# Unread products on TensorE ahead of and inside the lead of block attention

## The chip, the cores and the metric

One core of one Trainium2 chip. The metric is device time of one execution in microseconds (us), as the median of several runs. The kernel before took 1211.43 us (median of 3, from 1207.39 to 1212.15).

## The reference

Two transformer layers on x of shape (2, 1024, 128), each an attention and a feed-forward part behind a layer norm, with residual additions. The first layer has 16-head rotary attention and a mixture of eight experts chosen by argmax. The second is where the change lies:

```python
q = (hidden @ Wq.T + bq).reshape(B, S, 16, 8)          # k and v likewise; B, S = 2, 1024
scores = einsum('bihd,bjhd->bhij', q, k) / sqrt(8)
blk = arange(S) // 32
allowed = blk[:, None] >= blk[None, :]
scores = where(allowed, scores, 0)                     # zero, not minus infinity
probs = softmax(scores, axis=-1)
ctx = einsum('bhij,bjhd->bihd', probs, v)
x = x + ctx @ Wo.T + bo                                # then a gated feed-forward part
```

Masked scores are 0, so each row's softmax has a share from later keys, which the kernel takes from suffix sums of the values.

## The kernel before, in words

The kernel runs three functions one after the other: `rotary_attention` (to some 714 us), `experts`, and `block_attention` (from about 823 us). Engines have their own instruction streams and meet only by semaphores and at the ends of a `Block`.

`block_attention` has two blocks. The first normalizes x, projects it with Wq, Wk and Wv in eight 512-column products (`project`, L1175) and four quarters of values (`project_v`, L1183), and sums values for the later keys (`sum_values`). On TensorE (PE) its last work is `project_v(3)`, at k = 7 of the loop at L1200. VectorE (DVE) still splits k into a high and a low part, adds the value bias and scales the sums (`keep_sums`, L1300) before the block ends.

The second block holds the attention proper, in 8 groups of 4 heads (2 batches by 4). Each group has 20 fills and 24 steps. A fill is a pair of score blocks, for two heads, with queries on the partitions: `query_scores(f, 0)` and `(f, 1)` (L1536), products on 61 or 64 rows, the first head's in partitions 0 to 63, the second's in 64 to 127, each into one of three 512-column PSUM banks. DVE takes the row maximum of each bank (`row_max`, L1744, the reduction at L1754) and frees it; a fill may not start before the bank of three blocks ago is free (L1545). The maxima give each row's shift, which goes back through PE transposes (`shift_transposes`, L1501), ScalarE (ACT) and small transfers of SyncE (SP) into the moving operand. A step is a pair of score blocks with keys on the partitions (`key_scores`, L1512), of which ACT takes the exponential (`exps`, L1693, L1700); after two of four steps PE multiplies them with the values (`values`, L1562, L1575), four heads side by side in the bank `out_ps`, and at the end of a half adds the suffix product (L1579).

Every engine goes through the same list of jobs j = -1 to 207. Fills run ahead of steps by LEAD = 22 fills. So j = -1, the lead, is 22 fills with nothing else on PE but eight transposes ahead of fill 12:

```python
def fills_at(j):
    return range(0, LEAD) if j < 0 else range(fills_by(j - 1), fills_by(j))
```

From j = 0 on, the order within a job is key scores, fills, then at j = 5, 9, 13, ... two values products.

`fixed` is a constant f32 table of 128 partitions in SBUF; `w_ps` is a PSUM bank of the first block, read last when the normalized x of quarter 2 is kept; `out_ps` is first written by `values(0, 0)` with start=True.

Of the kernel before, what the change touches and what calls it, by code (L numbers as in the profile page):

```python
# [10 lines left out]
P = 128  # L11
# [1031 lines left out]
def block_attention(nc, core, operands, q_rows, k_rows, W_r, W_k, W_v, mu_r, mu_k, out):  # L1043
# [6 lines left out]
    with ExitStack() as st:  # L1050
# [4 lines left out]
        suffix, fixed = operands.suffix, operands.fixed  # L1055
# [18 lines left out]
        def sum_values(to, b):  # L1074
# [5 lines left out]
                                           start=kt == 4 * half, stop=kt == TB - 1)  # L1080
            return ins

        def keep_sums(src, b):

            own = fixed[:, 640:768].rearrange("p (h d) -> p h d", h=H1)
            for half in range(2):
                ins = nc.vector.tensor_tensor(suffix[:, b, half, :, 0:DH1], src[:, half * P:half * P + P].rearrange("p (h d) -> p h d", h=H1), own, ALU.mult)
            return ins
# [19 lines left out]
        with ExitStack() as st2:  # L1108
# [7 lines left out]
            w_ps = ps2("w", [P, 512])  # L1116

            def transpose_weights(pe):
                pe.wait_ge(operands.weights_loaded, 64)
                for i in range(4):  # L1120
                    ins = nc.tensor.transpose(w_ps[:, i * D:i * D + D], w[:, i, :], core.ident[:])
                ins.then_inc(wT_ready, 1)
# [21 lines left out]
            with nc.Block() as block:  # L1144
                @block.sync
                def _(sp):
                    sp.wait_ge(stack_ready, 2)
                    store_rows(sp, 0, 0, slice(0, HG), q_stored[0])
                    sp.wait_ge(stack_ready, 4)
                    store_rows(sp, 1, 0, slice(0, HG), k_stored[0])  # L1150
                    sp.wait_ge(q_stored[0], STORED)
                    load_pair(sp, q_still[0], q_rows, 0, 0, first_loaded[0])
                    sp.wait_ge(k_stored[0], STORED)
                    load_pair(sp, k_cur[0], k_rows, 0, 0, first_loaded[0])
                    load_pair(sp, q_still[0], q_rows, 0, 1, first_loaded[1])
                    load_pair(sp, k_cur[0], k_rows, 0, 1, first_loaded[1])
                    load_moving(sp, 0)
# [6 lines left out]
                @block.tensor  # L1164
                def _(pe):
                    def turn_normed(b):
                        for q in (2 * b, 2 * b + 1):
                            pe.wait_ge(xn_ready, q + 1)
                            if q == 3:
                                pe.wait_ge(full_ready, 1)  # L1170
                            for t in range(4 * q, 4 * q + 4):
                                ins = nc.tensor.transpose(turned_ps[q][:, t % 4 * P:t % 4 * P + P], xn[:, t, :], core.ident[:])
                            ins.then_inc(xnT_ready, 1)

                    def project(k):  # L1175
                        i, c = ORDER[k]
                        if k % 4 < 2:
                            pe.wait_ge(xT_kept, c + 1)
                        if k >= DEPTH:
                            pe.wait_ge(full_ready, k - DEPTH + 1)  # L1180
                        nc.tensor.matmul(s_ps[k % DEPTH][:], w_T[:, i, :], core.xT[:, c * 512:c * 512 + 512], start=True, stop=True).then_inc(proj_ready, 1)

                    def project_v(q):  # L1183
                        if q >= 2:
                            pe.wait_ge(v_added, q - 1)
                        for t in range(4 * q, 4 * q + 4):
                            ins = nc.tensor.matmul(v_ps[q % 2][:, t % 4 * D:t % 4 * D + D], core.xT[:, t * P:t * P + P], w_T[:, 2, :],
                                                   start=True, stop=True)
                        ins.then_inc(v_ready, 1)

                    transpose_weights(pe)
                    turn_normed(0)
                    pe.wait_ge(wT_copied, 1)
                    for k in range(4):
                        project(k)
                    for q in range(2):
                        project_v(q)
                    turn_normed(1)
                    pe.wait_ge(xT_kept, 4)
                    for k in range(4, 2 * DEPTH):  # L1200
                        project(k)
                        if k == 5:
                            pe.wait_ge(operands.fixed_loaded, 16)
                            pe.wait_ge(v_added, 2)
                            sum_values(sums_ps, 0).then_inc(sums_ready, 1)
                        if k >= 6:
                            project_v(k - 4)

                @block.scalar
                def _(act):  # L1210
# [112 lines left out]
        out_ps = ps("out", [P, 512])  # L1323
# [28 lines left out]
        def live(j):  # L1352

            return 0 <= j < GROUPS * STEPS
# [5 lines left out]
        def fills_at(j):  # L1360

            return range(0, LEAD) if j < 0 else range(fills_by(j - 1), fills_by(j))
# [71 lines left out]
        def fill_of(f, x):  # L1434
            m, i = f // FILLS, f % FILLS
            kind, hp = (i % 4, i // 4) if i < 8 else (i // 2, i % 2)
            return m, KINDS[kind], hp, x

        with nc.Block() as block:
# [60 lines left out]
            def _(pe):  # L1500
# [35 lines left out]
                def query_scores(f, x):  # L1536
                    m, (t, lo, hi), hp, x = fill_of(f, x)
                    n = bank["fill", f, x]
                    if m == 0 and f in (0, 4) and x == 0:
                        pe.wait_ge(operands.first_loaded[hp], LOADED)  # L1540
                    if m and f % FILLS == 0 and x == 0:
                        pe.wait_ge(still_loaded[m % 2], LOADED * (m // 2 + m % 2))
                        pe.wait_ge(k_loaded[m % 3], LOADED * (m // 3 + (m % 3 > 0)))
                    if n >= 3:
                        pe.wait_ge(bank_free, n - 2)  # L1545
                    parts = [(t, lo, hi, 0)]
                    if t < 2:
                        parts.append((t + 4, 4, t + 5, (hi - lo) * P))
                    for t, lo, hi, at in parts:
                        own = hi == t + 1  # L1550
                        rest = (hi - lo - own) * P
                        if rest:
                            rows = slice(64 * x, 64 * x + 61)
                            ins = nc.tensor.matmul(score_ps[n % 3][:, at:at + rest], q_still[m % 2][hp][rows, t * P:t * P + P],  # L1554
                                                   k_cur[m % 3][hp][rows, lo * P:lo * P + rest], start=True, stop=True)
                        if own:
                            rows = slice(64 * x, 64 * x + 64)
                            ins = nc.tensor.matmul(score_ps[n % 3][:, at + rest:at + rest + P], q_still[m % 2][hp][rows, t * P:t * P + P],  # L1558
                                                   k_cur[m % 3][hp][rows, t * P:t * P + P], start=True, stop=True)
                    ins.then_inc(bank_filled, 1)  # L1560
# [91 lines left out]
                for j in JOBS:  # L1652
                    if live(j):
                        key_scores(j)
                    for f in fills_at(j):
                        if shift_at(f):
                            shift_transposes(*shift_at(f))
                        if f < GROUPS * FILLS:
                            query_scores(f, 0)
                            query_scores(f, 1)  # L1660
                    if j % 4 == 1 and live(j - 5):
                        for k in range(2):
                            values((j - 5) // STEPS, (j - 5) % STEPS // 2 + k)
                    if j == SUMS_AT:
                        sum_later_values()
                    if turned(j):
                        turn(*turned(j))
                    if projected(j, 0):
                        transpose_attn(*projected(j, 0))
                    if projected(j, 1):  # L1670
                        project(*projected(j, 1))
                    if j == WEIGHTS_AT:
                        turn_weights()
                    for q in due(TURN_X, j):
                        turn_x(q)
                    for q in due(KEYS, j):
                        key(q)
                    for q in due(RECEPTANCE, j):
                        receptance(q)
                    for q in due(VALUES, j):  # L1680
                        value(q)
# [341 lines left out]
```

## Time and profile before

| | |
|---|---|
| median of 3 runs | 1211.43 us |
| profiled execution, own time | 1209.21 us |
| its span | 1207.1 us |
| mean granted clock of PE | 0.942 of 2.4 GHz |
| PE busy | 1080.6 us (90%) |
| DVE busy | 931.7 us (77%) |
| ACT busy | 695.9 us (58%) |

The span is the time between the first and last recorded work, about 2.1 us less than the execution's time. Busy PE isn't PE at its peak: at a lower granted clock the same products are busy longer. The granted clock is given as a fraction, 1.00 being 2.4 GHz and 0.50 being 1.2 GHz. A slice is 30.2 us.

### The profile page before, as it was taken

What the parts mean: (1) busy time and instruction counts of PE and PEld (TensorE: products, weight loads), DVE (VectorE), ACT (ScalarE), POOL (GpSimd) and SP (SyncE); (2) the same over time, 40 slices, a digit from 0 to 9 for tenths busy, and PEclk for the clock granted to TensorE, in tenths of its full rate; (3) what the DMA queues carried; (4) which work ended last, traced back from release to release, by engine and by line L of the source; (5) the groups of instructions that cost most, each with busy time, mean ns of one, the idle gap of its engine ahead of it and who ended that gap; (6) DMA issues with size and microseconds to landing.
All of it is one profiled execution on the core that took longest, in us unless ns stands there. A gap on an engine that the chain in (4) does not pass through costs nothing. (4 is left out here: it accounts for less than half of the span.)

```text
span 1207.1 us, 33673 instructions
## 1 busy us (share of the span) xinstructions
PE 1080.6 (90%) x13115; PEld 623.6 (52%) x13115; DVE 931.7 (77%) x1453; ACT 695.9 (58%) x1324; POOL 363.8 (30%) x240
## 2 busy tenths in 40 slices
PE   3899999999999999999999984876899999999885
PEld 2345554554554555455455463863655654555443
DVE  6888888989888898898988885337857676666767
ACT  3567666676666766667666664643146564555652
POOL 0442552463354255246335422770000000000000
PEclk9999999999999999999999996896669999998998
DMA  6866665556555666555655554213533111110001
GB/s 177 224 146 147 151 140 142 136 132 163 139 136 129 150 151 138 144 139 129 160 139 140 129 152 139 60 51 94 168 123 124 48 33 44 48 54 20 1 2 35
DMA packets 65866, 138.14 MB, mean 114 GB/s; under 512 B 13217, under 2 KB 33602, under 8 KB 61714
## 3 DMA queue, kind: packets, MB, share of 16 engines
q1 hardware_dynamic: 63954, 132.87, 43.3%
q0 software_dynamic: 1856, 4.52, 1.3%
q8 instruction: 34, 0.56, 0.2%
q14 instruction: 22, 0.18, 0.0%
HBM read 62.77 MB, written 22.41 MB: 71 GB/s over the span
## 5 line engine op out<-in xcount | busy, mean ns | idle before, releaser
L482 ACT ACTIVATE a_probs<-a_score,a_negmax 128x1024 f32<-128x1024 f32 x256 | 285.2, 1114 | 247.3 <-DVE a_negmax L567 247.3
L567 DVE TENSOR_REDUCE a_negmax<-a_score 128x1 f32<-128x1024 f32 x256 | 309.6, 1209 | 90.6 <-PE a_score L362 90.1
L1754 DVE TENSOR_REDUCE a_lowest<-a_score 128x1 f32<-128x512 f32 (+3 forms) x320 | 181.8, 630 | 75.4 <-PE a_score L1558 37.7
L1700 ACT ACTIVATE a_probs_T<-a_score_T 128x1024 f32<-128x1024 f32 (+1 forms) x192 | 146.7, 810 | 136.6 <-PE a_score_T L1532 95.3
L328 POOL TENSOR_TENSOR residual<-residual,a_scaled 128x512 f32<-128x512 f32 x62 | 79.0, 1275 | 333.9 <-ACT a_scaled L494 333.9
L573 DVE STREAM_TRANSPOSE a_probs_Tb<-a_probs 128x1024 f32<-128x1024 f32 x128 | 156.9, 1226 | 0.1
L573 DVE STREAM_TRANSPOSE a_probs_Ta<-a_probs 128x1024 f32<-128x1024 f32 x128 | 156.9, 1226 | 0.0
L362 PE MATMUL a_score<-a_k_halvesa,a_q_twicea 64*128 64x512 f32 x512 | 142.0, 642 | 13.1 <-DMA a_k_halvesa<-a_k_turned 11.2
L362 PE MATMUL a_score<-a_k_halvesb,a_q_twiceb 64*128 64x512 f32 x512 | 140.5, 635 | 1.2 <-ACT a_probs L482 1.1
L374 PE MATMUL a_acc<-a_probs_Ta,a_v_repa 32*64 32x256 f32 x4096 | 131.0, 382 | 4.3 <-ACT a_scaled L494 3.9
L374 PE MATMUL a_acc<-a_probs_Tb,a_v_repb 32*64 32x256 f32 x4096 | 126.3, 380 | 1.8 <-ACT a_scaled L494 1.8
L374 PEld LDWEIGHTS a_acc<-a_probs_Ta,a_v_repa 32*64 32x64 f32 x4096 | 84.4, 131 | 76.3 <-issue 66.0
L374 PEld LDWEIGHTS a_acc<-a_probs_Tb,a_v_repb 32*64 32x64 f32 x4096 | 87.7, 131 | 58.4 <-issue 34.1
L1554 PE MATMUL a_score<-a_k_cur,a_q_still 61*128 61x512 f32 (+3 forms) x320 | 106.2, 434 | 6.9 <-DVE a_lowest L1754 5.3
L1497 POOL COPY a_v_pad<-a_v_den 128x288 f32<-128x288 f32 x8 | 3.6, 453 | 289.1 <-PE a_out L1579 289.1
L313 POOL TENSOR_TENSOR shared<-shared,a_tables 128x1024 f32<-128x1024 f32 x32 | 75.8, 2369 | 45.9 <-DMA shared<-shared 45.9
L1575 PE MATMUL a_out<-a_probs_T,a_v_pad 128*32 128x512 f32 (+3 forms) x768 | 82.1, 549 | 0.2 <-ACT a_probs_T L1700 0.2
L349 PE MATMUL a_acc<-a_xn_cur,a_w_cur 128*128 128x512 f32 x128 | 68.2, 634 | 10.3 <-ACT a_attn_T L488 10.3
L1532 PE MATMUL a_score_T<-a_q_moving,a_k_cur 61*128 61x512 f32 (+3 forms) x320 | 70.7, 392 | 7.1 <-ACT a_probs_T L1700 7.1
L314 POOL TENSOR_TENSOR shared<-shared,a_tables 128x1024 f32<-128x1024 f32 x32 | 75.8, 2368 | 0.0
L362 PEld LDWEIGHTS a_score<-a_k_halvesa,a_q_twicea 64*128 64x128 f32 x512 | 40.4, 187 | 64.2 <-issue 41.8
L1554 PEld LDWEIGHTS a_score<-a_k_cur,a_q_still 61*128 61x128 f32 x320 | 55.1, 206 | 34.0 <-DVE a_lowest L1754 25.9
(257 smaller groups left out, 1431.2 us busy)
## 6 DMA issues: line engine op xcount, KB each, us to landing
shared<-shared SPq DMA_DIRECT2D x136, 128.0 KB, 2.3
a_v_repa<-rows_v SPq DMA_DIRECT2D x64, 256.0 KB, 4.4
a_v_repb<-rows_v SPq DMA_DIRECT2D x64, 256.0 KB, 4.7
a_xn_cur<-normed_T SPq DMA_DIRECT2D x17, 512.0 KB, 3.3
rows_v<-a_v_stage SPq DMA_DIRECT2D x68, 128.0 KB, 2.4
a_q_twicea<-a_q_turned SPq DMA_DIRECT2D x32, 256.0 KB, 3.4
a_q_twiceb<-a_q_turned SPq DMA_DIRECT2D x32, 256.0 KB, 3.3
a_k_halvesa<-a_k_turned SPq DMA_DIRECT2D x32, 128.0 KB, 3.6
```

The costliest lines, as they stand in the source:

```text
L313: nc.gpsimd.tensor_tensor(raw[i][:], raw[i][:], tables[:, 0, :], ALU.mult).then_inc(rotated[i], 1)
L314: nc.gpsimd.tensor_tensor(rot[i][:], rot[i][:], tables[:, 1, :], ALU.mult).then_inc(rotated[i], 1)
L328: nc.gpsimd.tensor_tensor(rows, rows, scaled[j][:], ALU.add).then_inc(added, 1)
L362: last = nc.tensor.matmul(score_ps[s % 2][:, half * 512:half * 512 + 512], q_twice[h][rows, tile * P:tile * P + P], k_halves[h][rows, :], ...
L374: ins = nc.tensor.matmul(acc_ps[64 * c:64 * c + 64, a, 0:TB * 32], v_rep[h][rows, v_block, :], probs_T[h][rows, block_, :], start=i == 0, ...
L482: nc.scalar.activation(probs[s % 2][:], score_ps[s % 2][:], ACT.Exp, bias=negmax[:, s:s + 1], accum_out=den[:, s:s + 1]).then_inc(probs_re ...
L567: nc.vector.tensor_reduce(negmax[:, s:s + 1], score_ps[s % 2][:], axis=AX.X, op=ALU.max, negate=True)\
L573: nc.vector.transpose(out=probs_T[h][:, :, 32 * tile:32 * tile + 32], in_=probs[s % 2][:].rearrange("p (b k) -> p b k", b=KB))\
L1554: ins = nc.tensor.matmul(score_ps[n % 3][:, at:at + rest], q_still[m % 2][hp][rows, t * P:t * P + P], k_cur[m % 3][hp][rows, lo * P:lo * P ...
L1575: ins = nc.tensor.matmul(out_ps[32 * h:32 * h + 32, lo - 512 * half:512], v_pad[:, kt, h, :], probs_T[n % 4][:, h, 0:hi - lo], start=kt == ...
L1700: nc.scalar.activation(probs_T[k % 4][:, 2 * hp:2 * hp + 2, 0:hi - lo], score_T_ps[n % 2][:, :, 0:hi - lo], ACT.Exp).then_inc(pair_free, 1)
L1754: nc.vector.tensor_reduce(to, src, axis=AX.X, op=ALU.max, negate=True).then_inc(bank_free, 1)
```

## The change

Two places gain matmuls whose results nobody reads. Each is an f32 product of a 128 x 128 stationary operand and 512 moving columns from `fixed`, with no wait and no semaphore of its own.

```diff
+        def keep_busy(to):
+            nc.tensor.matmul(to[:], fixed[:, 0:P], fixed[:, 0:512], start=True, stop=True)
...
                         if k >= 6:
                             project_v(k - 4)
+                    for _ in range(4):
+                        keep_busy(w_ps)
...
                         if f < GROUPS * FILLS:
                             query_scores(f, 0)
                             query_scores(f, 1)
+                            if j < 0:
+                                keep_busy(out_ps)
```

The first place adds four products at the end of PE's part of the first block. The second adds one behind each of the 22 fills of the lead. Nothing is removed or moved.

## Rows read from the trace of the kernel before

**Rows 1.** The page's slices: TensorE busy and granted clock in tenths, 40 equal slices.

```profile
PE   3899999999999999999999984876899999999885
...
PEclk9999999999999999999999996896669999998998
```

**Rows 2.** Windows cut where the clock changes: busy us per engine (instructions), clock, DMA share, GB/s.

```profile
841.00:851.40 10.40, 7.83 (x56) 6.23 (x54) 5.90 (x13) 3.02 (x5) 1.26 (x3) 0.99 0.54 163
851.40:895.80 44.40, 42.92 (x192) 29.48 (x195) 34.03 (x71) 10.96 (x15) 1.12 (x3) 0.50 0.53 178
895.80:1008.40 112.60, 102.09 (x891) 58.88 (x884) 77.30 (x165) 67.68 (x95) 1.36 (x3) 1.00 0.20 65
1008.40:1011.90 3.50, 3.50 (x17) 0.92 (x19) 1.29 (x2) 1.17 (x3) 0.00 (x0) 0.51 0.01 4
```

**Rows 3.** Timeline at the block change: start, length, engine, line, what, count, idle before.

```profile
837.87 3.64 PE L1181 MATMUL a1p_s_ps<-normed_T,a1p_w_T 128*128 128x512 f32 x4 [0.69 <-ACT normed_T L1214]
844.01 1.02 PE L1181 MATMUL a1p_s_ps<-normed_T,a1p_w_T 128*128 128x512 f32 x2
844.88 1.05 PE L1187 MATMUL a1p_v_ps<-a1p_w_T,normed_T 128*128 128x128 f32 x8
...
849.40 0.48 DVE L1087 TENSOR_TENSOR a_suffix<-a1p_sums_ps,a_fixed 128x128 f32<-128x128 f32 x2
...
850.18 0.44 PE L1558 MATMUL a_score<-a_k_cur,a_q_still 64*128 64x128 f32 x4 [2.50 <-PEq L1144]
```

**Rows 4.** One line by itself, min/median/max ns: weight loads of the value projection.

```profile
L1187 PEld LDWEIGHTS a1p_v_ps<-a1p_w_T,normed_T x32: 190/192/192, 832.6 to 847.3; 128*128 128x128 f32 x32
```

**Rows 5.** Windows of the lead, of steps 0 to 9, and of one thin stretch.

```profile
850.20:876.90 26.70, 25.54 (x89) 18.11 (x90) 23.98 (x51) 2.47 (x3) 2.32 (x5) 0.52 0.54 171
878.60:897.10 18.50, 18.12 (x109) 11.13 (x109) 9.40 (x21) 8.49 (x12) 0.00 (x0) 0.53 0.46 172
877.00:887.00 10.00, 9.62 (x60) 8.27 (x60) 5.64 (x12) 5.73 (x8) 0.00 (x0) 0.50 0.11 31
1005.10:1008.40 3.30, 1.98 (x12) 1.18 (x13) 1.85 (x4) 3.30 (x5) 0.00 (x0) 1.00 0.00 0
```

**Rows 6.** Groups by shape on VectorE in the lead: busy and mean ns, idle before.

```profile
L1754 DVE TENSOR_REDUCE a_lowest<-a_score 128x2 f32<-128x256 f32 x4 | 1.5, 417 | 0.0
```

**Rows 7.** Timeline of VectorE in the lead.

```profile
861.11 3.67 DVE L1754 TENSOR_REDUCE a_lowest<-a_score 128x1 f32<-128x512 f32 x6
...
866.39 9.18 DVE L1754 TENSOR_REDUCE a_lowest<-a_score 128x1 f32<-128x512 f32 x16 [1.61 <-PE a_score L1554]
```

**Rows 8.** Timeline of TensorE in group 2, full clock.

```profile
955.14 0.86 PE L1575 MATMUL a_out<-a_probs_T,a_v_pad 128*32 128x256 f32 x16
...
956.79 0.33 PE L1527 MATMUL a_score_T<-a_q_moving,a_k_cur 64*128 64x128 f32 x2
...
960.99 0.66 PE L1588 MATMUL a_score<-ident,normed_T 128*128 128x128 f32 x4
...
969.24 0.40 PE L1554 MATMUL a_score<-a_k_cur,a_q_still 61*128 61x512 f32 x2
```

**Rows 9.** Timeline of ScalarE: exponentials of steps 0, 10, 14 in groups 0, 2, 3.

```profile
878.59 2.73 ACT L1700 ACTIVATE a_probs_T<-a_score_T 128x1024 f32<-128x1024 f32 x3 [10.43 <-PE a_score_T L1532]
...
897.13 1.02 ACT L1700 ACTIVATE a_probs_T<-a_score_T 128x1024 f32<-128x1024 f32 x1 [2.64 <-PE a_score_T L1532]
...
954.78 1.94 ACT L1700 ACTIVATE a_probs_T<-a_score_T 128x1024 f32<-128x1024 f32 x2 [1.02 <-PE a_score_T L1532]
...
969.44 1.02 ACT L1700 ACTIVATE a_probs_T<-a_score_T 128x1024 f32<-128x1024 f32 x1 [1.95 <-PE a_score_T L1532]
...
977.22 2.85 ACT L1700 ACTIVATE a_probs_T<-a_score_T 128x1024 f32<-128x1024 f32 x3 [2.24 <-PE a_score_T L1532]
...
989.57 1.94 ACT L1700 ACTIVATE a_probs_T<-a_score_T 128x1024 f32<-128x1024 f32 x2 [1.02 <-PE a_score_T L1532]
...
1013.60 2.85 ACT L1700 ACTIVATE a_probs_T<-a_score_T 128x1024 f32<-128x1024 f32 x3 [3.75 <-PE a_score_T L1532]
```

## The prediction

> **What bounds the kernel now.** I read the slices first: where TensorE (PE) and VectorE (DVE) are busy, and the granted clock under them. PE is at 8 or 9 tenths nearly throughout. The clock line stands at 9, and falls to 6 in four slices; the last two of them, 845 to 905 us, are where block attention's scores begin, and PE is at 9 under them: busy at a reduced clock [rows 1]. I then cut the span at the points where the clock changes. From 851.4 to 895.8 us, 44.4 us long, the clock is 0.50 (1.2 GHz); before it 10.4 us at 0.99, behind it 112.6 us at 1.00 (2.4 GHz); behind that come single dips, as the 3.5 us from 1008.4 at 0.51 [rows 2]; the scattered 8s at the end of the clock line are more of them [rows 1]. What PE did before the fall: its last product of the projection stage was done at 847.7, it stood 2.50 us idle at the change of block, then ran only small score pieces [rows 3]. This hole is all the change can get at.
>
> The hole has two parts with different limits. The lead (22 pairs of score blocks, 850.2 to 876.9) belongs to DVE: 24.0 us busy of 26.7 [rows 5], the timeline has strings of row maxima such as sixteen in 9.18 us [rows 7], which the chain of waits names too, and PE waits for DVE to give back banks. A half-speed PE costs little there. The second part, steps 0 to 9 of group 0, belongs to PE: 18.12 busy of 18.5 us, DVE 9.40 [rows 5]. There the clock is the time.
>
> **Part one, the four products behind the last projection.** They start at about 847.6 (850.18 less the 2.50 idle is the end of the last recorded product, 847.7), where PE stands idle [rows 3]. One f32 product of 128 x 512 is two recorded instructions; at the full clock the pair at 844.01 is followed by the next work at 844.88, 0.87 us later [rows 3]. Four take 3.5 us and end at about 851.1. The block now ends with DVE's last instruction at 849.88 (849.40 + 0.48), and the next begins 0.30 us later at 850.18 [rows 3]. What was hidden idle time is used up, and PE becomes the last into the block change: 851.1 + 0.3 - 850.18 = 1.2 us later if the change waits for the products to finish, 0.75 if PE only queues behind its own stream. I take +1.0. Everything of the lead, its maxima on DVE and the loads and stores that SP issues at the block's start, moves with it; these transfers have slack (first needed some 20 us later), so they add nothing more. What it buys: PE has no pause from 841 on, so the cause of the fall at 851.4 is gone.
>
> **Part two, the 22 products of the lead.** At the full clock they are 22 x 0.87 = 19.1 us of new PE work. A pair of score blocks asks PE for 0.2 us (both halves of the rows side by side) to 0.40 us (one recorded block of 512 at the full clock [rows 8]), so a pair with its product takes PE 1.07 to 1.27 us. DVE takes 1.20: six maxima in 3.67 us are 0.60 apart [rows 7]. PE and DVE are thus level, and only just. Bounds for the lead: below, DVE keeps the lead and the gaps in which it waited (1.61 us behind the shift transposes [rows 7], 2.7 us in all by its busy share [rows 5]) shrink, about -2. Above, PE is the bound: 22 x 1.27 + 1.0 for the eight shift transposes (four others take 0.66 at the full clock, tails included [rows 8]) = 28.9 against 26.7 now, +2.2. The narrow blocks speak for the upper part: of 256 columns DVE needs only 0.42 us for one [rows 6], a pair 0.84 at most, and PE 1.07. The last product also stands ahead of step 0's scores. I take +1.0.
>
> One rule of the Trainium skill speaks against this part. The row first: eight matmuls of the value projection, all on 128 rows, take 1.05 us [rows 3], while the weight load of each takes 0.19 [rows 4], eight of them 1.5; the loads must lie beside running matmuls of the same rows, and beside each other. TensorE: Matmul & The Clock Gate, in Part 3 (Packing small matmuls), says that a weight load overlaps a running matmul "only when row_grp differs". By that rule each product would expose two loads, 22 x 2 x 0.19 = 8.4 us. The trace disagrees here, so this is a rival, not a term.
>
> **What the clock gives back.** Steps 0 to 9 exist at both clocks. In group 0 (half clock) the exponential of step 0 starts at 878.59 and that of step 10 at 897.13: 18.54 us. In group 2 (full clock) they start at 954.78 and 969.44: 14.66 [rows 9]. So at least 3.9 us. Group 2 carries work in that stretch that group 0 doesn't have: values and suffix of the group before it, 955.14 to 956.79, 1.65 us, and four transposes of 0.66 at 960.99 [rows 8]. Upper bound 3.9 + 1.65 + 0.66 = 6.2. PE isn't the limit at every point, so I take 5.0. This holds if the clock stays up, and nothing of the change stands in those steps: the added products end with the lead. Steps 0 to 4 of group 0 are poor in PE work, with no values until step 5. The one dip shown stands behind such a thin stretch: 1005.1 to 1008.4 has PE 1.98 busy of 3.3 us [rows 5], and the clock is 0.51 in the next 3.5 [rows 2]. I therefore expect one dip. Its price: from the first exponential to step 14 group 2 takes 977.22 - 954.78 = 22.4 us, group 3 with the dip 1013.60 - 989.57 = 24.0; 1.6 us [rows 9]. Net gain 5.0 - 1.6 = 3.4.
>
> **Sum.** +1.0 + 1.0 - 3.4 = -1.4 us. The profiled execution took 1209.21 us (span 1207.1 and 2.1 around it), 2.2 below the median of the three runs, 1211.43. Own time of the changed kernel by that execution 1207.8; against the median 1210.0, which I give.
>
> **Rivals.**
> - The clock holds right through. Then the sum is 1.0 + 1.0 - 5.0 = -3.0, 1208.4. For it: 112.6 us of steady stage ran through without a fall [rows 2]. Against: every later group has values products of the group before it in its first steps, group 0 has none. With every term at its good end (0.75 - 2 - 6.2) it is -7.5, 1204.
> - The gain is lost behind the lead: the clock falls in steps 0 to 4 and comes back about where it does now, since nothing there differs from before. Only some 0.8 us of steps 0 and 1 is won, and 2.0 paid: +1.2, 1212.6. For it: at half clock PE was 9.62 busy of 10.0 us in 877 to 887 [rows 5] and the clock still rose only at 895.8 [rows 2]. Against: the dip at 1008.4 lasted 3.5 us. The Trainium skill, in Part 4 (PE-mode transpose) of the same page, says that transposes do not count as PE-busy for the clock; eight stand at step 2, which would make this rival likelier. No row here separates them from other work.
> - PE becomes the bound of the lead. It decides where a pair with its product exceeds DVE's 1.20 us; by the rows it is at most 1.27. If each product exposes its two weight loads of 0.19, the pair is 1.45 to 1.65 and the lead 8.4 us longer: -1.4 + 8.4 = +7.0, 1218.4.
> - The lead runs at the half clock all the same. Two products at 837.87, at half clock, took 3.64 us, twice the full clock's 0.87 each with the tail [rows 3]. A product of 1.74 and a pair's 0.43 make 2.17 us against DVE's 1.20: 22 x 0.97 = +21 in the lead, +1 ahead of it, and nothing won behind: about 1233. Against: behind just those two products back to back the clock was 0.99 [rows 2, 3], so the added ones should lift it even if it fell.
>
> **Chances.** One dip, 0.38. Clock holds, 0.25. Lost behind the lead, 0.20. PE the bound by its loads, 0.05. Lead at half clock, 0.03. The rest, 0.09, is the later groups: a shift of a microsecond moves where the dips fall, each worth 1.6 us either way. Half a per cent, 6 us, is about what a measurement can tell from no change here. Faster by more needs nearly all good ends or lost dips later, 0.10; slower by more is the last two rivals and some ill luck, 0.10; within, 0.80. The range: 1204.5 from the holding clock's good ends, 1217.0 short of the weight-load rival, with the spread of the runs before inside.
>
> **What the profile of the changed kernel would show.** The product group behind the projection ends near 851, and the first score starts 0.75 to 1.2 us later than 850.18: part one. The granted clock is 1.00 from 841 to the end of the lead: without it the whole reading is wrong. The lead (first score to the first exponential, now 850.18 to 878.59, 28.4 us) takes 27 to 31: part two; above 34 means loads are exposed. First exponential to that of step 10 in group 0: 13.5 us if the clock held, 15 with a dip, 17 or more if the gain was lost. Group 2 onward keeps its lengths of 35 to 39 us. The prediction is wrong if the time moves by more than 6 us either way, or if the lead, not the steps behind it, is where time changes.

## The result, and the profile of the changed kernel

| | before | changed |
|---|---|---|
| median | 1210.13 us (20 runs, 1202.41 to 1218.92) | 1216.53 us (20 runs, 1210.13 to 1223.18) |
| ratio | | 1.0046, 95% interval 1.0027 to 1.0064 |
| profiled span | 1207.1 us | 1215.7 us |
| mean granted clock | 0.942 | 0.953 |

The change makes the kernel slower by 0.46%, 5.6 us (3.3 to 7.7); the medians lie 6.4 apart. The clock is higher and the time longer.

The slices of the changed kernel answer to [rows 1]: the slices at a granted clock of 6 where block attention's scores begin are gone.

```profile
PE   3899999999999999999999983957989999999885
...
PEclk8899999999999999999999995988998989999997
```

Windows of the changed kernel, columns as in [rows 2]. From 832.0 to 910.4 us the clock is 1.00. In the lead (second row) PE is busy 34.49 of 34.5 us and VectorE 26.70; before, 25.54 of 26.7 and 23.98 [rows 5]. The lead has changed owner. The short half-clock stretches come after it.

```profile
832.00:851.10 19.10, 17.00 (x86) 10.98 (x85) 12.51 (x31) 8.44 (x15) 0.04 (x1) 1.00 0.53 137
851.10:885.60 34.50, 34.49 (x144) 14.52 (x146) 26.70 (x53) 2.48 (x4) 2.34 (x5) 1.00 0.44 139
885.60:899.20 13.60, 11.71 (x112) 7.01 (x110) 9.35 (x20) 8.18 (x12) 0.00 (x0) 1.00 0.43 151
899.20:910.40 11.20, 9.32 (x68) 4.88 (x65) 7.51 (x15) 8.75 (x11) 0.00 (x0) 1.00 0.50 200
910.40:913.80 3.40, 3.40 (x17) 0.59 (x16) 1.15 (x2) 0.46 (x1) 0.00 (x0) 0.50 0.73 298
```

The timeline at the block change, against [rows 3]. The four products (eight recorded, 3.60 us) outlast VectorE's last instruction at 849.57, and the first score comes 4.79 us after the start of the last value projection (846.32); before it came 3.55 us after it (846.63 to 850.18). That is +1.24 us.

```profile
846.32 1.05 PE L1191 MATMUL a1p_v_ps<-a1p_w_T,normed_T 128*128 128x128 f32 x8
...
847.21 3.60 PE L1085 MATMUL a1p_w_ps<-a_fixed 128*128 128x512 f32 x8
...
849.09 0.48 DVE L1091 TENSOR_TENSOR a_suffix<-a1p_sums_ps,a_fixed 128x128 f32<-128x128 f32 x2
...
851.11 0.44 PE L1564 MATMUL a_score<-a_k_cur,a_q_still 64*128 64x128 f32 x4 [0.30 <-PEq L1148]
```

One cycle of the lead: PE's matmuls, its weight loads (PEld) and the maxima on VectorE. Scores start at 866.11, the product at 866.56, the next scores at 867.62, the next product at 868.05. A pair takes 1.49 us, 0.43 for the scores and 1.06 for the product. The product's columns take 0.86: a product is two recorded instructions, and where products follow each other these start 0.43 apart. The other 0.20 is lost where PE passes between work on 128 rows and on 64, half of it on the way in and half on the way out, as the single records further down show. The weight loads of the scores start with them, at 867.62, and not beside the running product. The banks don't explain it: the first maximum of a pair starts 0.53 us behind its scores (867.62 to 868.15), so the pair of 866.11 gave its first bank back at about 866.64 + 0.68 = 867.3. VectorE takes two maxima and waits 0.2 us for the next pair; before, it had six in a row without a pause [rows 7].

```profile
866.11 0.52 PE L1560 MATMUL a_score<-a_k_cur,a_q_still 61*128 61x512 f32 x2
...
866.56 1.12 PE L1085 MATMUL a_out<-a_fixed 128*128 128x512 f32 x2
867.62 0.19 PEld L1560 LDWEIGHTS a_score<-a_k_cur,a_q_still 61*128 61x128 f32 x2 [0.76 <-DVE a_lowest L1762]
867.62 0.50 PE L1560 MATMUL a_score<-a_k_cur,a_q_still 61*128 61x512 f32 x2
868.05 0.30 PEld L1085 LDWEIGHTS a_out<-a_fixed 128*128 128x128 f32 x2 [0.25 <-issue]
868.05 1.12 PE L1085 MATMUL a_out<-a_fixed 128*128 128x512 f32 x2
868.15 1.29 DVE L1762 TENSOR_REDUCE a_lowest<-a_score 128x1 f32<-128x512 f32 x2 [0.23 <-PE a_score L1560]
```

The single records, from narrow windows of the same timeline:

```profile
867.09 0.59 PE L1085 MATMUL a_out<-a_fixed 128*128 128x512 f32 x1
868.05 0.19 PEld L1085 LDWEIGHTS a_out<-a_fixed 128*128 128x128 f32 x1 [0.25 <-issue]
868.58 0.59 PE L1085 MATMUL a_out<-a_fixed 128*128 128x512 f32 x1
868.59 0.09 PEld L1514 LDWEIGHTS a_score_T<-ident,a_shift_rows 128*8 128x8 f32 x1 [0.24 <-issue]
869.01 0.27 PE L1514 MATMUL a_score_T<-ident,a_shift_rows 128*8 128x128 f32 x1
```

A product's second instruction starts 0.53 us behind its first (868.05 to 868.58), 0.10 more than its columns, and the first weight load starts with the product, not ahead of it. The next scores start 0.52 behind the second instruction (867.09 to 867.62), 0.09 more. All 22 products of the lead show the same 0.53, and the 20 that scores of a fill follow directly the same 0.52. A shift transpose, which works on 128 rows like the product, starts 0.43 behind it (868.58 to 869.01), with its load beside the running product (868.59): there nothing is lost.

The chain of waits has PE's own work piece after piece:

```profile
864.70 0.43 PE a_score L1560 x2
865.13 1.05 PE a_out L1085 x2
866.18 0.45 PE a_score L1560 x2
866.63 1.05 PE a_out L1085 x2
```

The exponentials of steps 0 and 10 in group 0, against [rows 9]: 899.20 - 885.59 = 13.61 us where it was 18.54.

```profile
885.59 2.64 ACT L1708 ACTIVATE a_probs_T<-a_score_T 128x1024 f32<-128x1024 f32 x3 [13.01 <-PE a_score_T L1538]
...
899.20 1.02 ACT L1708 ACTIVATE a_probs_T<-a_score_T 128x1024 f32<-128x1024 f32 x1 [1.94 <-PE a_score_T L1538]
```

The profiled spans differ by 8.6 us. Block by block, from the first row maximum and the exponentials: first maximum at 851.55 against 850.63, +0.9; lead up to the first exponential 34.0 against 28.0, +6.1; steps 0 to 9 -4.9; steps 10 to 23 of group 0 23.4 against 20.1, +3.3; groups 1 to 7 266.2 against 263.0, +3.2; the end 0. The two +3 entries are short half-clock stretches: 11 behind step 9 of group 0 against 6.

### The profile page after: what moved, and what is told of

The parts are those of the page before. It is cut to its first block and busy times, and to the rows that moved or that the text cites. A ratio compares the mean times of both kernels' runs of the same rounds, so it can differ in the third digit from the quotient of the medians.

```text
span 1215.7 us, 33777 instructions
## 1 busy us (share of the span) xinstructions
PE 1091.6 (90%) x13167; PEld 616.5 (51%) x13167; DVE 933.4 (77%) x1453; ACT 696.1 (57%) x1324; POOL 364.3 (30%) x240
## 5 line engine op out<-in xcount | busy, mean ns | idle before, releaser
L1560 PE MATMUL a_score<-a_k_cur,a_q_still 61*128 61x512 f32 (+3 forms) x320 | 91.8, 397 | 6.1 <-DVE a_lowest L1762 4.6
L1581 PE MATMUL a_out<-a_probs_T,a_v_pad 128*32 128x512 f32 (+3 forms) x768 | 86.2, 572 | 0.2 <-ACT a_probs_T L1708 0.2
L1538 PE MATMUL a_score_T<-a_q_moving,a_k_cur 61*128 61x512 f32 (+3 forms) x320 | 68.1, 382 | 7.2 <-ACT a_probs_T L1708 7.1
L1560 PEld LDWEIGHTS a_score<-a_k_cur,a_q_still 61*128 61x128 f32 x320 | 46.4, 187 | 40.8 <-DVE a_lowest L1762 32.4
```

What stands on the lines that cost most here:

```text
L1538: ins = nc.tensor.matmul(score_T_ps[n % 2][:, x, off:hi - lo], k_cur[m % 3][hp][rows, kt * P:kt * P + P], q_moving[m % 2][hp][rows, lo + o ...
L1581: ins = nc.tensor.matmul(out_ps[32 * h:32 * h + 32, lo - 512 * half:512], v_pad[:, kt, h, :], probs_T[n % 4][:, h, 0:hi - lo], start=kt == ...
```

## The experiments

They ran on three chips: four_only, lead_only, lead_256 and lead_halves on one, after_again, lead_double, two_halves and two_halves_steps on the second, lead_f32r and two_halves_256 on the third. There the kernel before has medians of 1228.5, 1226.6 and 1230.1 us, 16 to 20 more than 1210.13, and in the profiles block attention begins 15 to 20 us later than before's 823.9. All ratios are to the kernel before on the same chip; it was profiled on none of the three. "Lead" is from the first row maximum to the first exponential, "steps" from that to step 10's, "dips" counts half-clock stretches behind it, without the last two, which stand at the end of every profile; each number is from the one profile of that kernel.

| kernel | lead us | steps us | dips | ratio (95%) |
|---|---|---|---|---|
| before (first chip) | 28.0 | 18.5 | 6 | 1 |
| the change (first chip) | 34.0 | 13.6 | 11 | 1.0046 (1.0027 to 1.0064) |
| after_again | 34.0 | 15.3 | 7 | 1.0008 (0.9979 to 1.0037) |
| four_only | 27.8 | 17.4 | 4 | 0.9974 (0.9947 to 1.0002) |
| lead_only | 37.1 | 13.6 | 6 | 1.0015 (0.9991 to 1.0040) |
| lead_256 | 28.1 | 15.2 | 5 | 0.9976 (0.9951 to 1.0002) |
| lead_halves | 28.3 | 15.3 | 8 | 0.9956 (0.9928 to 0.9983) |
| lead_double | 52.8 | 13.6 | 4 | 1.0117 (1.0066 to 1.0168) |
| lead_f32r | 35.5 | 13.6 | 4 | 1.0006 (0.9974 to 1.0038) |
| two_halves | 28.3 | 13.6 | 4 | 0.9941 (0.9912 to 0.9970) |
| two_halves_steps | 28.2 | 14.3 | 8 | 0.9973 (0.9948 to 0.9998) |
| two_halves_256 | 26.2 | 15.3 | 7 | 0.9918 (0.9888 to 0.9947) |

**Each part alone.** four_only:

```diff
-                            if j < 0:
-                                keep_busy(out_ps)
```

> Keeps the four products behind the last projection, leaves out the 22 of the lead. Theory (the lead's products are what costs; a thin lead lets the clock fall anyway): the first row maximum starts about 1.2 us later than before relative to the last projection, the lead is 27 to 28 us again, the clock falls to 0.50 inside the lead and stays there as before, steps 0 to 9 take 18 to 18.5 us; time +1 us, ratio 1.001. Rival (the pause at the block change alone caused the long fall): the clock stays at 1.00 through the lead, steps 0 to 9 take about 13.6 us, time -4 us, ratio 0.997.

Its windows: with no pause at the block change the clock held into the lead, and fell 3.3 us behind the first maximum (870.02) all the same, for 37.5 us.

```profile
860.00:873.30 13.30, 12.56 (x71) 8.60 (x70) 8.31 (x17) 2.77 (x5) 2.37 (x5) 1.00 0.68 197
873.30:910.80 37.50, 35.98 (x154) 24.82 (x154) 27.31 (x58) 8.92 (x13) 0.00 (x0) 0.50 0.45 144
910.80:930.00 19.20, 16.66 (x129) 8.08 (x128) 13.45 (x28) 12.40 (x15) 0.00 (x0) 1.00 0.50 202
```

The thin scores of the lead let the clock fall; the pause only set when. The theory's mechanism held, its time didn't: 1.001 lies just outside the interval of 0.9974. The profile has steps of 17.4 us, under the 18 expected, and 4 dips, and groups 1 to 7 take 259.9 us where before has 6 dips and 263.0. With +1.2 at the block change and -1.1 in the steps that comes to about -3, the measured size, but the dips of groups 1 to 7 make up nearly all of it.

lead_only leaves out the other part:

```diff
-                    for _ in range(4):
-                        keep_busy(w_ps)
```

> Keeps the 22 products of the lead, leaves out the four ahead of it. Theory: nothing is added at the block change, the clock falls once near its start and the full products bring it back within about 7 us, in which a pair costs some 2.6 us instead of 1.48; lead 35 to 38 us, steps 0 to 9 13.6 us, time +3 to +6 us, ratio about 1.004, like the change itself. Rival (the half clock persists once it is there): lead above 50 us, time +20 us.

The clock fell at 868.4 and was back at 875.2, and the lead was 37.1 us.

```profile
860.00:868.40 8.40, 5.90 (x38) 3.88 (x36) 4.15 (x10) 2.00 (x3) 2.05 (x5) 1.00 0.70 199
868.40:875.20 6.80, 6.80 (x16) 2.51 (x14) 3.60 (x6) 0.00 (x0) 0.33 (x1) 0.50 0.98 326
875.20:904.00 28.80, 28.80 (x117) 11.90 (x118) 22.35 (x45) 2.51 (x4) 0.00 (x0) 1.00 0.26 78
```

So the lead's products bring the clock back by themselves. The four ahead of them are worth 3.1 us of lead (37.1 against 34.0) and cost 1.2. The ratio, 1.0015, can be told neither from 1 nor from the 1.004 expected.

**The product's length.** lead_256:

```diff
-                                keep_busy(out_ps)
+                                nc.tensor.matmul(out_ps[:, 0:256], fixed[:, 0:P],
+                                                 fixed[:, 0:256], start=True, stop=True)
```

> As the change, but each product of the lead has 256 columns instead of 512. Theory (PE is the bound of the lead by a product's 0.85 us of columns plus 0.2 us until the next scores can start, and 0.43 us for the scores): 0.43 + 0.2 + 0.43 = 1.06 us a pair, under DVE's 1.20, so DVE bounds the lead again: 26 to 28 us instead of 34.0, the clock stays at 1.00, steps 0 to 9 take 13.6 us, time 6 us below the change and 3 to 4 us below before, ratio 0.997. Rival (256 columns are too little work to hold the clock): it falls in the lead, steps 0 to 9 take 18 us, ratio 1.002.

Half the columns brought the lead from 34.0 to 28.1 us, and the clock held through it. Product start to score start is 0.63 us (877.68 to 878.31): 0.43 of columns and again 0.20. The ratio is as forecast; the steps had one dip.

```profile
877.68 0.70 PE L1668 MATMUL a_out<-a_fixed 128*128 128x256 f32 x2
878.31 0.64 PE L1560 MATMUL a_score<-a_k_cur,a_q_still 61*128 61x512 f32 x2
```

lead_double puts two products behind each pair (`keep_busy(out_ps)` twice).

> The change with two products behind each pair of the lead instead of one. Theory (PE is the bound of the lead, so each further product of the same shape costs its columns, 0.85 us, and no second turn of 0.2 us): a pair takes 2.34 us instead of 1.48, the lead 34.0 + 22 x 0.86 = 53 us, time +19 us on the change. Rival (part of the lead's lengthening is waiting on VectorE): lead 48 us or less. Rival (each product brings its own turn and loads): 57 us.

52.8 us, forecast 53. Four recorded matmuls and the turn (so I call the 0.20, in and out together) take 894.72 to 896.63, 1.91 us = 4 x 0.43 + 0.20: one turn per pair, not per product. The bank that the next scores need had been free since 895.52 there, 1.1 us, and the 0.20 was the same, so it isn't a wait on VectorE. The time missed: 14.8 us above after_again by the medians (two runs only), not 19; the profile has 4 dips against 7.

```profile
894.72 1.98 PE L1085 MATMUL a_out<-a_fixed 128*128 128x512 f32 x4
896.63 0.50 PE L1560 MATMUL a_score<-a_k_cur,a_q_still 61*128 61x512 f32 x2
```

**What the 0.2 us is.** lead_halves keeps columns and type and takes the product in two pieces of 64 rows:

```diff
-                                keep_busy(out_ps)
+                                for x, to in enumerate((score_T_ps[1][:, 0, :], score_T_ps[1][:, 1, :])):
+                                    rows = slice(64 * x, 64 * x + 64)
+                                    nc.tensor.matmul(to, fixed[rows, 0:P], fixed[rows, 0:512],
+                                                     start=True, stop=True)
```

> As the change, but each product of the lead is two products on 64 rows each, side by side like the scores, with the same columns and type. Theory (what makes a pair 1.48 us instead of 1.27 is the turn between work on 128 rows and work on 64 rows): the 0.2 us behind a product goes, a pair takes 0.85 + 0.43 = 1.28 us or less, lead 28 to 30 us instead of 34.0, time 4 to 5 us below the change. Rival (the turn comes from the change of type f32 to f32r, or from waiting): pair stays at 1.48 and lead at 34 us, time as the change, ratio 1.005.

28.3 us, VectorE busy 25.54 of them. The turn is gone, and more: work of one half now runs beside work of the other. The scores of 877.85 run beside a product that starts at 877.95, and three recorded products take 1.03 us together, where three behind each other would take 2 x 0.43 + 0.59 = 1.45. This lets the pair follow VectorE's 1.20 us.

```profile
877.85 0.50 PE L1560 MATMUL a_score<-a_k_cur,a_q_still 61*128 61x512 f32 x1
877.95 1.03 PE L1670 MATMUL a_score_T<-a_fixed 64*128 64x512 f32 x3
```

lead_f32r holds the rows at 128 and changes the type:

```diff
-                                keep_busy(out_ps)
+                                for _ in range(4):
+                                    nc.tensor.matmul(out_ps[:], k_cur[2][0][:, 0:P],
+                                                     k_cur[2][0][:, 0:512], start=True, stop=True)
```

> As the change, but each f32 product of the lead is four f32r products of the same 128 rows and 512 columns (an idle key tile as operand): the same 2048 columns of streaming, 0.85 us, in the type of the scores. Theory (the 0.2 us behind a product comes from passing between work on 128 rows and on 64 rows): a pair stays at about 1.48 us, the lead at 34 us. Rival (it comes from the change of type between f32 and f32r): a pair takes 1.28 us, the lead 29 us. Rival (each f32r product brings loads that are not hidden): above 1.6 us, lead above 36.

The pair is 1.56 us (884.83 to 886.39), a little over the theory's 1.48, and the lead 35.5. The four products start at 885.25, 885.59, 885.83 and 886.07, the next scores at 886.39: 0.34, 0.24, 0.24 and 0.32 us. Against the 0.24 between products of this type the first interval is 0.10 longer and the last 0.09, the same turn of 0.20; the rest of the lengthening is that these four stand 0.24 apart, a little more than a fourth of 0.86. The type is not the cause of the turn; of the two differences between product and scores, the rows remain.

```profile
884.83 0.49 PE L1560 MATMUL a_score<-a_k_cur,a_q_still 61*128 61x512 f32 x2
885.25 1.21 PE L1669 MATMUL a_out<-a_k_cur 128*128 128x512 f32 x4
885.59 0.40 PE L1669 MATMUL a_out<-a_k_cur 128*128 128x512 f32 x1
886.07 0.40 PE L1669 MATMUL a_out<-a_k_cur 128*128 128x512 f32 x1
886.39 0.49 PE L1560 MATMUL a_score<-a_k_cur,a_q_still 61*128 61x512 f32 x2
```

The profile writes f32 for both types in these lines; the lines with x1 are single records of the four in the line with x4. An estimate for the whole pair follows. The scores are f32r too; with 0.24 for their 512 columns, the 0.43 that they hold PE leaves another 0.20. So a pair would be 0.86 + 0.24 of columns and about 0.40 for two changes of rows, 1.50 against the 1.49 measured.

**The change once more.**

> The changed kernel itself once more, beside the versions below. Theory (the lead is 6.1 us longer, the block change 1.2 us, steps 0 to 9 are 4.9 us shorter, and later dips of the clock are as many as before on the mean): +2.4 us, ratio 1.002. Rival (the change also brings more dips in later groups, 11 against 6 in the two profiles, 1.6 us each): +5 to +8 us, ratio 1.004 to 1.006, as first measured.

Lead and block change repeat to the hundredth (34.03 us, PE busy 34.10 of 34.1). The steps took 15.3 us with a dip at 907.8, and 7 dips followed instead of 11, from the same kernel on another chip. The ratio 1.0008 fits the theory's 1.002 and leaves the rival's 1.004 out only barely. Its interval holds 1: on this chip the change can't be told from no change.

**Towards a better version.** two_halves is lead_halves with `range(2)` in place of `range(4)`.

> As the version with two 64-row products per pair, with two products instead of four behind the last projection. Theory (two end before VectorE does, so the block change costs nothing, and PE's pause is too short to let the clock fall): first score 1.2 us earlier relative to the last projection than with four, lead 28 us, clock 1.00 through it, steps 0 to 9 13.6 to 15.3 us; time -4 to -5 us, ratio 0.996. Rival (two leave too long a pause): the clock falls at the lead's start for one 3.4 us stretch, lead 30 to 31 us, ratio 0.998.

The last projection starts at 862.77 and the first score at 866.33, 3.56 us as in the kernel before, and the clock is 1.00 through the lead:

```profile
863.70:866.80 3.10, 2.32 (x12) 1.04 (x12) 2.32 (x7) 0.00 (x0) 0.51 (x2) 1.00 0.62 194
866.80:895.00 28.20, 27.60 (x186) 18.68 (x185) 25.51 (x53) 2.47 (x3) 1.86 (x5) 1.00 0.53 170
```

The ratio is 0.9941, 7.2 us. Steps 4.9 us shorter and, by the profiles, 3.2 in groups 1 to 7 with 4 dips for 6 make up that size. two_halves_steps adds one 128-row product of 256 columns behind each fill of steps 0 to 4:

> As two_halves, with one more 128-row product of 256 columns behind each fill of steps 0 to 4 (four in all). Theory (steps 0 to 4 are where the clock dips, and PE has room there): no dip in steps 0 to 9, 13.6 to 14.5 us, ratio 0.995. Rival (PE is the bound there too, each product costs its 0.63 us): steps 0 to 9 take 15.5 to 16.5 us, ratio 0.997.

No dip in the steps, 14.3 us against 13.6 without one and 15.3 with one; the ratio 0.9973 gives no reason to keep it. two_halves_256 halves the columns of the 64-row products (`0:256` in both operands and the outputs):

> As two_halves, with 256 columns per 64-row product instead of 512. Theory (VectorE already bounds the lead at 28.3 us with 512 columns, so fewer columns win nothing there, and half the work still holds the clock, as the 128-row products of 256 columns did): lead 27 to 28 us, steps 0 to 9 13.6 to 15.3 us, ratio 0.994 like two_halves. Rival (too little work in the lead to hold the clock): the clock falls in the lead, steps 0 to 9 take 17 to 18 us, ratio 0.998 to 1.000.

```profile
867.20:893.40 26.20, 24.04 (x186) 17.93 (x185) 25.21 (x53) 2.48 (x4) 1.87 (x5) 1.00 0.58 183
893.40:900.10 6.70, 5.08 (x52) 4.06 (x54) 4.14 (x8) 5.58 (x8) 0.00 (x0) 1.00 0.01 2
900.10:903.50 3.40, 3.40 (x21) 0.85 (x20) 1.05 (x3) 0.00 (x0) 0.00 (x0) 0.50 0.76 223
```

The lead is 26.2 us, and VectorE is busy 25.21 of them: I had expected nothing from fewer columns. 0.9918 is the best measured, about 10 us (6.5 to 13.8); it can't be told from two_halves, whose interval overlaps. Its lead is 1.8 us shorter than before's and its steps 3.3. That is 5 of the 10; what the rest is stays open, since the kernel before has no profile on that chip.

## Why the prediction was wrong

It gave -1.4 us, 1204.5 to 1217.0, with 0.80 on no measurable change. The measured change is +5.6 us, clear of zero, on the other side. The median itself, 1216.53, still lies inside the range, at its upper end. Two of the prediction's own signs were met: the time changed in the lead, and the lead from first score to first exponential is 34.48 us (851.11 to 885.59), where it had said that above 34 means exposed loads.

- Block change: predicted +1.0 with 1.2 as its upper case; 1.24 measured. Right. The lower case of 0.75 doesn't follow from its numbers, 851.1 - 850.18 being 0.9.
- **The lead is the step that failed**: +1.0 taken, +2.2 as the upper bound, +6.1 measured. I took the product's price from a row where its neighbours have the same shape, 0.87 us [rows 3]; between 64-row scores it is 1.06. And I took 0.40 us, the recorded length of one block [rows 8], as the dearest case of a pair; with its own exposed loads it holds PE 0.43. The term that I put at nothing was the change of rows, twice a pair. Together 1.49 a pair against VectorE's 1.20, not 1.07 to 1.27. 22 x 0.29 = 6.4 us, about the 6.1 lost. lead_double, lead_256 and lead_halves confirm it from three sides.
- The third rival, PE as the bound by two exposed loads per product, named the place, the point of decision (1.20 us) and a pair of 1.45 to 1.65 us, and had a chance of 0.05. It was what happened in the lead (+6.1 against its +9.4), though not by its mechanism in detail: the product's second load lies beside its running first half. What is exposed is the product's first load and the loads of the scores behind it, one at each change of rows. The Trainium skill, TensorE: Matmul & The Clock Gate, Part 3, says that weight loads overlap running matmuls "only when row_grp differs". I set it aside because same-row loads overlap in the trace, which they do (a transpose's at 868.59 beside the product); I read no row in which the number of rows changes. The trace of the kernel before has such places at the full clock. One is in group 2 and stands below: the shift transposes, on 128 rows, start 0.11 apart, and the scores behind them 0.20 (957.98 to 958.18). The price the rival gave, 0.38 us a product, was near the 0.22 to 0.42 by which the pair exceeded my two ends.

```profile
957.87 0.27 PE L1508 MATMUL a_score_T<-ident,a_shift_rows 128*8 128x128 f32 x1
957.98 0.27 PE L1509 MATMUL a_score_T<-ident,a_later_rows 128*128 128x128 f32 x1
958.18 0.45 PE L1554 MATMUL a_score<-a_k_cur,a_q_still 61*128 61x384 f32 x2
```

- What the clock gives back: 5.0 without a dip, 3.4 with one; measured 4.9 in the change's first profile, 3.3 in the second (15.27 us). Right for steps 0 to 9, with "clock 1.00 to the end of the lead". But the first profile has two dips right behind them, and over all 24 steps of group 0 it gives back only 1.6 us (13.6 + 23.4 against 18.5 + 20.1), the second 3.3.
- Sum of what was repeated: 1.2 + 6.1 - 4.9 (or 3.3) = +2.4 to +4.0 us. The first measurement has +5.6 (3.3 to 7.7), the second +1.0 (-2.6 to +4.5). The interval of each holds some part of it. Whether the change also makes dips in later groups more frequent on the first chip, as 11 against 6 suggest, stays open: the same kernel showed 11 and 7.

## What to carry to other kernels

Price filler work at the place where it will stand: take a row in which its neighbours have the shape that they will have there, and test the sum against the period of the engine that now sets the pace; 0.29 us over it, 22 times, ate all that the clock returned. Give filler the tile shape of the work around it, and only as many columns as hold the clock. Look for the places in the trace where the work already changes shape: their gaps give its price. Where an engine idles until another finishes, as PE did for 2.5 us at the block change, filler that ends before that is free (two products), and what sticks out costs one to one (the four, 1.24 us).

## What the runs showed of the hardware that I had not expected

- Between a 64-row matmul and a 128-row product something was lost both ways: the first recorded part of the product lasted 0.10 us longer than its columns, with its weight load not ahead of it, and the scores behind it started 0.09 late, 0.20 together, the same for f32 (`after`) and f32r (lead_f32r). Between matmuls on 128 rows there was no such gap (0.43 us apart, the columns), also with another operand and width behind.
- 64-row products and 64-row scores on different halves of the array ran beside each other, also of different types (lead_halves, 877.85 and 877.95).
- In four_only the scores alone did not hold the clock, though it was 1.00 when they began: it fell 3.3 us behind the first maximum. Products of 256 columns on 64 rows, twice per pair, held it for 26.2 us.
- The short dips in the steady stage are not a property of the program alone: 11 and 7 in two profiles of one kernel, 4 to 8 in its relatives. They go with the 13 us by which its runs spread: of the 20, the fastest (1210.13 us) has a mean granted clock of 0.961, the slowest (1223.18) 0.948.
